# Fills of a down projection on half-height tiles, all four scores of a step ahead of them, in the last 16 attention steps of a transformer layer

## What is computed

```
xn = layernorm(x)
attn: q,k,v = sign-linear(xn); scores = q k^T / 4; softmax; out = attn v; sign-linear(out)
ffn:  hidden = silu(xn @ gate.T) * (xn @ up.T);  out_flat = hidden @ down.T
x + attn(xn) + ffn(xn)
```

## Time and profile before

| | us |
|---|---|
| median of 3 runs | 510.2 |
| the runs | 509.6, 510.2, 514.09 |
| profiled execution, its own time | 510.75 |
| its span | 509.0 |
| PE busy in the span | 485.1 (95%) |
| DVE busy | 417.5 (82%) |
| ACT busy | 352.6 (69%) |
| POOL busy | 93.3 (18%) |

### The profile page before, as it was taken

One profiled execution on the slowest core, in us unless ns is written; L12 is line 12 of the kernel. 1 busy time (PEld: TensorE's weight loads), 2 busy tenths in 40 slices (PEclk: granted clock), 3 DMA queues, 4 the chain that ended last, 5 costly groups with the idle time before them and its releaser, 6 DMA issues.

```text
span 509.0 us, 9735 instructions
## 1 busy us (share of the span) xinstructions
PE 485.1 (95%) x3882; PEld 161.2 (32%) x3882; DVE 417.5 (82%) x487; ACT 352.6 (69%) x655; POOL 93.3 (18%) x138
## 2 busy tenths in 40 slices
PE   1899999998999999999999999999999999999996
PEld 1564434433332222222222222222222222223442
DVE  7879769675777999999999999999999952223985
ACT  1943634342228999999999999999999987774000
POOL 4212244434323000000000000000000103241021
PEclk9999999999998999999999999999999999999999
DMA  8944773731103702102101210220210204452311
GB/s 263 278 86 100 160 146 44 204 63 21 23 0 49 139 23 62 40 24 64 40 30 56 40 57 27 42 61 23 62 41 24 62 25 121 111 151 74 105 70 55
DMA packets 31300, 38.99 MB, mean 77 GB/s; under 512 B 6608, under 2 KB 20816, under 8 KB 31256
## 3 DMA queue, kind: packets, MB, share of 16 engines
q1 hardware_dynamic: 22232, 27.34, 18.8%
q0 software_dynamic: 8304, 10.95, 11.6%
q10 hardware_dynamic: 720, 0.08, 0.1%
HBM read 33.24 MB, written 10.35 MB: 86 GB/s over the span
## 4 chain that ended last, share of the span: by engine, by line
PE 75%; ACT 15%; DVE 4%; DMA 3%; issue 2%; SPq 1%; ACTq 0%; DVEq 0%
PE ps L1219 22%; PE ps L1091 15%; PE ps L1184 13%; ACT room L674 13%; PE ps L1152 10%; PE ps L1100 7%; PE ps L1070 3%; PE ps L1245 3%; DMA room<-wo_rows 2%; ACT osb L685 1%; DMA hlo<-x 1%; PE ps L1008 1%; DVE nmx L807 1%; PE ps L1062 1%; SPq L421 1%
## 5 line engine op out<-in xcount | busy, mean ns | idle before, releaser
L807 DVE TENSOR_REDUCE nmx<-ps 128x1 f32<-128x1024 f32 x256 | 293.6, 1216 | 14.4 <-PE ps L1100 14.1
L674 ACT ACTIVATE room<-ps 128x512 f32<-128x512 f32 x512 | 274.4, 597 | 22.0 <-PE ps L1184 12.1
L1219 PE MATMUL ps<-room,vcur 128*32 128x256 f32 (+1 forms) x1912 | 160.9, 408 | 4.4 <-ACT osb L685 4.1
L1184 PE MATMUL ps<-qst,kB 50*128 50x512 f16 x512 | 149.7, 384 | 0.8 <-DVE room L906 0.5
L1100 PE MATMUL ps<-kA,qst 48*128 48x512 f16 x512 | 145.7, 383 | 2.3 <-DVE sob L880 1.8
L1091 PE MATMUL ps<-room,wf 128*128 128x512 f16 x448 | 100.7, 380 | 0.0
L1219 PEld LDWEIGHTS ps<-room,vcur 128*32 128x32 f32 x1912 | 37.7, 108 | 100.5 <-issue 53.4
L1184 PEld LDWEIGHTS ps<-qst,kB 50*128 50x128 f16 x512 | 30.7, 93 | 112.5 <-ACT room L674 102.5
L655 ACT ACTIVATE room<-ps,gsc 128x512 f32<-128x512 f32 x28 | 19.2, 685 | 60.3 <-PE ps L1091 60.3
L1091 PEld LDWEIGHTS ps<-room,wf 128*128 128x128 f16 x448 | 42.4, 98 | 54.6 <-issue 6.6
L513 POOL TENSOR_TENSOR hlo<-room,hhi 128x512 f16<-128x512 f32 x28 | 34.0, 1216 | 90.0 <-ACT hhi L585 89.9
(11 more groups left out here) (127 smaller groups left out, 267.7 us busy)
## 6 DMA issues: line engine op xcount, KB each, us to landing
qst<-q_scratch SPq DMA_DIRECT2D x32, 192.0 KB, 3.6
o_scratch<-osb SPq DMA_DIRECT2D x16, 256.0 KB, 2.3
q_scratch<-parts SPq DMA_DIRECT2D x12, 256.0 KB
hlo<-x SPq DMA_DIRECT2D x8, 256.0 KB, 4.9
parts<-x POOLq DMA_DIRECT2D x8, 256.0 KB, 4.1
wf<-gate POOLq DMA_DIRECT2D x14, 128.0 KB, 4.2
wf<-up POOLq DMA_DIRECT2D x14, 128.0 KB, 6.1
wd<-down POOLq DMA_DIRECT2D x1, 1792.0 KB, 13.3
```

Source lines behind the costliest of these rows:

```text
L674: nc.scalar.activation(probs[:, s % 2, r, :], ps[:, score_bank(entry(j, i)), :], ACT.Exp, scale=gam_reg[par][r]).then_inc(scores_free, 1)
L807: nc.vector.tensor_reduce(nmx[:, hf, idx:idx + 1], bank_pair(idx % 2), AX.X, ALU.max, negate=True).then_inc(rows_free, 1)
L1184: nc.tensor.matmul(ps[:, score_bank(e), :], kB[low:low + SROWS, par, kt % (TT // 2) * P:(kt % (TT // 2) + 1) * P], qst[low:low + SROWS, pa ...
L1219: mm = nc.tensor.matmul(ps[32 * r:32 * r + 32, 7, of], vcur[:, par, key_tile(r, j), :], probs[:, s % 2, r, of], start=(j == 0 and part == ...
```

## The change

Only steps 16 to 31 of the last pair and what reads their banks change.

- A step's order on TensorE becomes four scores, seven fills, the values of the step before.
- A fill is now two matmuls, each over 64 of the 128 rows, the lower 64 rows into bank 0 and the upper 64 rows into bank 1 (`down_halves`). All four tiles use the same two banks one after the other, so that the first fill of tile 1, 2 and 3 waits on `halves_free`.
- `down_out` of these tiles takes three VectorE instructions in place of one: a copy of bank 0, the addition of bank 1 (which counts `halves_free`), the product with the scale.
- The four scores of a step have banks 4, 5, 6 and 3, and each waits for the exponential that last read its bank; the one in bank 3 also waits for all row maxima (`rows_free`). The one transpose of this stretch has bank 2.
- `out_proj` writes banks 2, 3, 0, 1 in place of 0 to 3, and its first four wait for those banks in place of waiting for `ff_ready`.

```diff
+    LATE_SCORES = [4, 5, 6, 3]
+    LATE_T = 2
+    FILL_BANKS = [0, 1]
+    O_BANK = [2, 3, 0, 1]
+    LATE = (NG - 1) * STEPS
...
             def down_out(i):
 
-                dve.wait_ge(down_ready, i + 1)
-                nc.vector.tensor_tensor(ffn[i], ps[:, i, :], dsb[:, :], ALU.mult).then_inc(ff_ready, 1)
+                if i < FILL:
+                    dve.wait_ge(down_halves_ready, 2 * (i + 1))
+                else:
+                    dve.wait_ge(down_ready, i - FILL + 1)
+                if i < FILL:
+                    nc.vector.tensor_copy(ffn[i], ps[:, FILL_BANKS[0], :]).then_inc(halves_step, 1)
+                    dve.wait_ge(halves_step, i + 1)
+                    nc.vector.tensor_tensor(ffn[i], ps[:, FILL_BANKS[1], :], ffn[i], ALU.add).then_inc(halves_free, 1)
+                    dve.wait_ge(halves_free, i + 1)
+                    nc.vector.tensor_tensor(ffn[i], ffn[i], dsb[:, :], ALU.mult).then_inc(ff_ready, 1)
...
-            def down_proj(i, f, part):
+            def down_halves(i, f, part):
 
                 if f == 0 and part == 0:
-                    if i < 4:
+                    if i == 0:
                         pe.wait_ge(wd_loaded, 16)
                         pe.wait_ge(rows_free, 2 + NG * 2 * UNITS)
-                    elif i < 7:
+                    else:
+                        pe.wait_ge(halves_free, i)
+                for b in range(2):
+                    low = b * HI
+                    mm = nc.tensor.matmul(ps[:, FILL_BANKS[b], :], (hhi, hlo)[part][low:low + HI, f, i * P:(i + 1) * P],
+                                          wd[low:low + HI, f, :], start=(f == 0 and part == 0),
+                                          stop=(f == FT - 1 and part == 1))
+                    if f == FT - 1 and part == 1:
+                        mm.then_inc(down_halves_ready, 1)
...
-                    pe.wait_ge(scores_free, block_ * BLOCK + exps_before(e) + 3)
-                    if e - 3 == T_ENTRY and transposes:
-                        pe.wait_ge(max_taken, block_ + 2)
+                    if step >= LATE:
+                        if LATE_SCORES[i] == 3:
+                            pe.wait_ge(rows_free, 2 + NG * 2 * UNITS)
+                        pe.wait_ge(scores_free, 3 + (step - 1) * REP + min(i + 1 + (step == LATE), REP))
+                    else:
+                        pe.wait_ge(scores_free, block_ * BLOCK + exps_before(e) + 3)
+                        if e - 3 == T_ENTRY and transposes:
+                            pe.wait_ge(max_taken, block_ + 2)
...
                         times_values(gp, s - 1, i // 2, 2)
-                    elif i == 1 and not with_rows:
-                        times_values(gp, s - 1, 0, 1)
                     elif i == REP - 1 and not with_rows:
                         for n in fill:
-                            down_proj(*FILLS[n])
+                            down_halves(*FILLS[n])
+                        times_values(gp, s - 1, 0, 1)
...
                 if i < FILL:
-                    pe.wait_ge(ff_ready, i + 1)
+                    if O_BANK[i] == LATE_T:
+                        pe.wait_ge(max_taken, 2 * NG)
+                    elif O_BANK[i] in FILL_BANKS:
+                        pe.wait_ge(halves_free, FILL)
+                    else:
+                        pe.wait_ge(scores_free, 3 + NG * STEPS * REP)
```

More of the change, by code:

```diff
@@ L121, in layer_kernel, with bank_of @@
     assert (BLOCK + 1) % 3 == 0
+    LATE_SCORES = [4, 5, 6, 3]
[3 more added lines that the diff above has]
+    LATE = (NG - 1) * STEPS
+    def bank_of(gp, s, i):
+        if gp * 2 * STEPS + s >= LATE:
+            return LATE_SCORES[i]
+        return score_bank(entry(s % TT, i))
     def exps_before(e):
@@ L320, in layer_kernel @@
         down_ready = sem("down_ready")
+        down_halves_ready = sem("down_halves_ready")
         oproj_ready = sem("oproj_ready")
@@ L323, in layer_kernel @@
         ff_ready = sem("ff_ready")
+        halves_step = sem("halves_step")
+        halves_free = sem("halves_free")
         res_loaded = [sem(f"res_loaded{i}") for i in range(3)]
@@ L669, in exps @@
                 if j == T_STEP + 1 and not (last and s >= STEPS + TT):
-                    take_max(gp * 4 + s // TT + 1, score_bank(T_ENTRY))
+                    take_max(gp * 4 + s // TT + 1, LATE_T if step >= LATE else score_bank(T_ENTRY))
                 act.wait_ge(probs_free, step + 1)
@@ L673, in exps @@
                     act.wait_ge(scores_ready, step * REP + i + 1)
-                    nc.scalar.activation(probs[:, s % 2, r, :], ps[:, score_bank(entry(j, i)), :], ACT.Exp,
+                    nc.scalar.activation(probs[:, s % 2, r, :], ps[:, bank_of(gp, s, i), :], ACT.Exp,
                                          scale=gam_reg[par][r]).then_inc(scores_free, 1)
@@ L960, in rows_out @@
                     dve.wait_ge(out_ready, i - 1)
-                nc.vector.tensor_tensor(att[:, i % 2, :], ps[:, i % FILL, :], sob[:, :], ALU.mult).then_inc(att_ready, 1)
+                nc.vector.tensor_tensor(att[:, i % 2, :], ps[:, O_BANK[i % FILL], :], sob[:, :], ALU.mult).then_inc(att_ready, 1)
                 dve.wait_ge(att_ready, 2 * i + 1)
@@ L1140, in _ @@
                     transpose_max(0, 0, 6)
+            def down_halves(i, f, part):
+                if f == 0 and part == 0:
+                    if i == 0:
+                        pe.wait_ge(wd_loaded, 16)
+                        pe.wait_ge(rows_free, 2 + NG * 2 * UNITS)
[8 more added lines that the diff above has]
+                        mm.then_inc(down_halves_ready, 1)
             def down_proj(i, f, part):
                 if f == 0 and part == 0:
-                    if i < 4:
-                        pe.wait_ge(wd_loaded, 16)
-                        pe.wait_ge(rows_free, 2 + NG * 2 * UNITS)
-                    elif i < 7:
+                    if i < 7:
                         pe.wait_ge(scores_free, 3 + NG * STEPS * REP)
@@ L1159, in scores @@
                 gp_, par, hf, j = at(gp, s)
+                step = gp * (2 * STEPS) + s
                 block_ = gp * 4 + s // TT
@@ L1178, in scores @@
                     e = entry(j, i)
-                    pe.wait_ge(scores_free, block_ * BLOCK + exps_before(e) + 3)
-                    if e - 3 == T_ENTRY and transposes:
-                        pe.wait_ge(max_taken, block_ + 2)
+                    if step >= LATE:
+                        if LATE_SCORES[i] == 3:
+                            pe.wait_ge(rows_free, 2 + NG * 2 * UNITS)
+                        pe.wait_ge(scores_free, 3 + (step - 1) * REP + min(i + 1 + (step == LATE), REP))
[3 more added lines that the diff above has]
+                            pe.wait_ge(max_taken, block_ + 2)
                     if opening and i == 2:
                         pe.wait_ge(h_ready, FU)
-                    nc.tensor.matmul(ps[:, score_bank(e), :],
+                    nc.tensor.matmul(ps[:, bank_of(gp, s, i), :],
                                      kB[low:low + SROWS, par, kt % (TT // 2) * P:(kt % (TT // 2) + 1) * P],
@@ L1197, in scores @@
                         times_values(gp, s - 1, i // 2, 2)
-                    elif i == 1 and not with_rows:
-                        times_values(gp, s - 1, 0, 1)
                     elif i == REP - 1 and not with_rows:
                         for n in fill:
-                            down_proj(*FILLS[n])
-                if j == T_STEP and transposes:
+                            down_halves(*FILLS[n])
+                        times_values(gp, s - 1, 0, 1)
+                if j == T_STEP and transposes and step < LATE:
                     pe.wait_ge(scores_free, block_ * BLOCK + exps_before(T_ENTRY) + 3)
                     transpose_max(block_ + 1, 1 - hf, score_bank(T_ENTRY))
+                elif j == T_STEP and transposes:
+                    transpose_max(block_ + 1, 1 - hf, LATE_T)
             def times_values(gp, s, part, cut):
@@ L1244, in out_proj @@
                     for part in range(2):
-                        mm = nc.tensor.matmul(ps[:, i % FILL, :], oparts[:, t, part, i * P:(i + 1) * P], sgno[:, t, :],
+                        mm = nc.tensor.matmul(ps[:, O_BANK[i % FILL], :], oparts[:, t, part, i * P:(i + 1) * P], sgno[:, t, :],
                                               start=(t == 0 and part == 0), stop=(t == QT - 1 and part == 1))
```

1 line of the change is left out of this document (added).

## The result

| | before | changed kernel |
|---|---|---|
| median, us | 510.2 | 520.68 |
| runs, us | 509.48 to 514.09 (5) | 520.56 to 524.71 (5) |
| ratio, 95% interval | | 1.0205, 1.017 to 1.024 |
| profiled execution and its span | 510.75 / 509.0 | 524.71 / 523.0 |

The change makes the kernel 2% slower, 10.5 us by the medians. The forecast was 516.9 with a range up to 520.2. Its direction was right, its size was not: the result lies half a microsecond above the range and 0.4 from the rival "all three waits drop the clock", 520.3.

What follows compares the result with a forecast made beforehand. TensorE was taken to bound steps 16 to 31 without a gap. -3.2 - 0.14 + 0.35 + 7.8 + 0.3 + 1.6 = +6.7 on 510.75 gave 517.5, forecast as a median of 516.9 us, range 513.9 to 520.2.

Steps and rivals of the forecast that it cites:

- all three waits drop the clock: Rival: TensorE's clock halves behind each wait at steps 20, 24 and 28; 3.4 above the forecast, 520.3 us; chance 0.12.
- Term 1: New order in steps 17 to 31: fewer switches, 3.03 to 3.04 us a step against 3.25, -3.2 us; end, -0.14.
- The rival of unpaired fills: Each pair of half-height fills shows 0.09 us of weight loading; net +8.2 on the forecast, 525 us; chance 0.04.
- Term 2: Entry at step 16: bank 3's score waits for the last row maxima, so step 17 begins later, +0.35 us.
- Term 3: Waits on `halves_free` at steps 20, 24, 28: 2.6 us each behind VectorE's queue, +7.8; block 3's reciprocal, +0.3.
- Term 4: TensorE's clock behind the three waits: a half-rate stretch costs 1.5 to 1.7 us; one of three taken, +1.6.
- The hidden parts: Tail: block 3's split and tile 3's copy and addition (1.4 us) stay covered; without that cover +0.7 us.
- The rival without waits: VectorE frees the banks by S + 3.6 (S: start of step 19's scores), no waits; -3.0, 507.2 us; chance 0.07.

Runs made afterwards that it cites:

- The two runs above: Changed kernel's order with full-height fills, tiles in banks 0, 1, 2, 0: 511.23 us; kernel before, old order, with half-height fills in two bank pairs: 509.66 us.

## Why the prediction was right and wrong

- **Term 1** held to the hundredth: 3.04 us a step (0.54 + 1.51 + 0.99), half fills pair at 0.216. The two runs above confirm its parts, half height and order. The rival of unpaired fills falls.
- **Term 2**: step 17 began 2.94 us after the last row maximum (418.06 to 421.00), against 2.42 before: +0.52 in place of +0.35, since the chain has 0.39 for the last score, where I had put 0.22.
- **Term 3** was right in place, cause and size. 6.05 us from the scores to the release in place of 6.18, idle 2.47 and with the 0.17 that the timeline does not show 2.64 in place of 2.6: +7.9 for +7.8. The copy took 0.68, the price that I took. Block 3's reciprocal cost nothing (460.34, while `o_low` waited for ScalarE until 463.68): 0 for +0.3.
- **Term 4** is the step that failed. "I take one of three" was mis-sized: all three waits brought the clock down, in both profiles, 4.8 us for +1.6. The price of one loss was right, 1.58 to 1.64 us against 1.5 to 1.7; their number was wrong. In front of me lay one stretch that lost the clock and one that did not. I set the odds at one in three, where waits of this length lose it in most cases. The rival "all three waits drop the clock" is what happened, and I had given it 0.12.
- **Sum**: -3.2 - 0.14 + 0.5 + 7.9 + 4.8 = +9.9, against 10.1 in the profiles' stretches and 10.5 by the medians.
- **The hidden parts** were hidden: the output projections ran without a gap behind 480.55. **The rival without waits** named its condition rightly, a release by S + 3.6; where VectorE met it, the waits went.

## What to carry to other kernels

When a change makes an engine wait for another's queue, count from that queue's order, not from how idle the engine is: VectorE was free here, and its position behind one waiting instruction cost 2.47 us three times. In a stretch like this one, price a standstill of TensorE of over 2 us at its length and another 1.5 to 1.6 us (it came in 9 of 11 here), and try moving entries of the queues before changing tiles or banks. An entry moved ahead is only safe if nothing that starts a transfer moves behind it.

## What the runs showed of the hardware

In the last 16 steps TensorE's clock went to 0.50 behind none of 3 waits of 0.80 us, not behind the one of 0.85, behind none of 3 of 1.14 or 1.15 and none of 2 of 1.75. It fell behind 7 of the 9 from 2.28 to 2.54. In both longer ones it had fallen some 0.4 us before the wait was over (at 461.2 and 461.7 us), and those cost 1.5 us beyond their length. Length alone does not decide. In the kernel before the clock also fell at 157.4 us, where the longest wait in the three microseconds ahead was 0.45 us, and it was at 1.00 behind one of 3.57 us at the very start (11.5 us). And the same wait of 1.83 us in the stage ahead (VectorE's `sob`, third row) is in all thirteen profiles, and 16 matmuls behind it took 3.63 us in seven of them and 5.31 in six. The timelines of before and of the changed kernel:

```profile
121.53 0.39 PE L1100 MATMUL ps<-kA,qst 48*128 48x512 f16 x2 [1.83 <-DVE sob L880]
121.85 3.63 PE L1091 MATMUL ps<-room,wf 128*128 128x512 f16 x16
```

```profile
122.17 0.39 PE L1126 MATMUL ps<-kA,qst 48*128 48x512 f16 x2 [1.83 <-DVE sob L896]
122.49 5.31 PE L1117 MATMUL ps<-room,wf 128*128 128x512 f16 x16
```

That is 1.7 us of difference between executions of the same instructions, and part of the 3.9 us ahead of the change. Of the rest, 1.5 us arise where both kernels begin the attention and the clock stood at 0.50 from 157.4 to 160.8 us before and from 160.4 to 167.2 in the changed kernel; 0.6 had arisen by 122 us. The Trainium skill, "TensorE: Matmul & The Clock Gate", section "What's actually happening", calls the gate's window free-running, so that the moment of a change varies from run to run. The six and seven agree with that; what decides in a single case no run here shows.
